# Keeping the bf16 parts of queries and keys in DRAM in the row order of the product

## The reference, cut to what matters

```
query = heads(ct_q @ Wu_q + b) + heads(rope(ct_q @ Wq_r + b))     # 16 heads of 8
key   = heads(ct_kv @ Wu_k + b) + heads(rope(x @ Wk_r + b))
value = heads(ct_kv @ Wu_v + b)
attn  = softmax(query @ key^T / 12)                               # no mask, 1024 x 1024 a head
out   = (attn @ value) @ Wo + b
```

## Time and profile before

| | |
|---|---|
| median of 3 runs | 2129.98 us (2129.47 to 2133.92) |
| the profiled execution's own time | 2124.84 us |
| span of that execution | 2123.1 us |
| busy: TensorE, VectorE, ScalarE, GpSimd | 86%, 69%, 52%, 30% of the span |
| mean granted TensorE clock | 0.939 of 2.4 GHz |
| maxima of the second attention | first at 1204.8 us, last at 1904.8 us |

### The profile page before, as it was taken

The page is one execution under the profiler, slowest core; times in us unless marked ns, Lnnn a source line. Parts: engine busy times, 40 slices in busy tenths (PEclk is TensorE's granted clock), DMA queues, the critical chain, the costliest instruction groups (busy, mean ns, idle before and its releaser), DMA issues. The chain is left out here.

```text
span 2123.1 us, 32719 instructions
## 1 busy us (share of the span) xinstructions
PE 1816.8 (86%) x12025; PEld 651.2 (31%) x12025; DVE 1473.0 (69%) x3100; ACT 1108.6 (52%) x1385; POOL 633.8 (30%) x771
## 2 busy tenths in 40 slices
PE   6455799999999999999599868888888888887899
PEld 3113333333333333333233312111211211112566
DVE  5874666666666666663344589999999899993543
ACT  4403244454444444445224248778877778885332
POOL 0031445554544454532025003303302400000152
PEclk9776699999999999999799969999999999999699
DMA  4000000000000000000021001111111111103114
GB/s 128 0 1 1 1 12 22 26 27 22 22 22 22 22 22 32 23 27 27 20 107 50 30 8 62 59 42 42 64 55 46 67 47 42 42 27 104 65 32 138
DMA packets 59451, 85.29 MB, mean 40 GB/s; under 512 B 21828, under 2 KB 38468, under 8 KB 59164
## 3 DMA queue, kind: packets, MB, share of 16 engines
q1 hardware_dynamic: 57724, 79.52, 11.1%
q0 software_dynamic: 1280, 2.62, 0.4%
q10 hardware_dynamic: 288, 1.05, 0.2%
HBM read 46.10 MB, written 32.22 MB: 37 GB/s over the span
## 5 line engine op out<-in xcount | busy, mean ns | idle before, releaser
L1575 DVE TENSOR_REDUCE h_m_half<-h_ps_max 128x1 f32<-128x512 f32 x1024 | 637.9, 682 | 53.1 <-PE h_ps_max L1284 49.0
L1460 ACT ACTIVATE h_P<-h_ps_st 128x1024 f32<-128x1024 f32 x512 | 497.7, 1023 | 103.8 <-PE h_ps_st L1300 101.2
L941 ACT ACTIVATE l_P<-l_ps_st 128x1024 f32<-128x1024 f32 (+3 forms) x384 | 306.6, 809 | 293.0 <-PE l_ps_st L821 292.0
L821 PE MATMUL l_ps_st<-l_Q,l_K 64*128 64x512 f32 (+3 forms) x1536 | 330.5, 510 | 1.2 <-DMA l_Q<-l_m_row 1.2
L1019 DVE CUSTOM_DVE_ANT_0 l_masked<-l_ps_t,l_mask 128x384 bf16<-128x384 f32 (+3 forms) x512 | 230.2, 487 | 79.5 <-PE l_ps_t L779 78.0
L1284 PE MATMUL h_ps_max<-h_K,h_Q 48*128 48x512 bf16 x1024 | 205.5, 398 | 78.3 <-DVE h_m_half L1575 75.2
L1310 PE MATMUL h_ps_o<-h_P,h_V 128*9 128x512 f32 x2048 | 271.8, 603 | 0.7 <-ACT h_P L1460 0.5
L1022 DVE TENSOR_REDUCE l_m_half<-l_ps_t 128x1 f32<-128x512 f32 x256 | 164.8, 685 | 97.1 <-PE l_ps_t L779 97.0
L990 POOL TENSOR_SCALAR_AFFINE_SELECT l_P<-l_P 128x256 f32<-128x256 f32 x256 | 102.8, 406 | 381.6 <-ACT l_P L941 381.2
L1300 PE MATMUL h_ps_st<-h_Q,h_K 51*128 51x512 bf16 x1024 | 169.8, 384 | 31.1 <-DMA h_Q<-h_m_row 18.4
L1284 PEld LDWEIGHTS h_ps_max<-h_K,h_Q 48*128 48x128 bf16 x1024 | 49.6, 93 | 404.3 <-DVE h_m_half L1575 385.9
(11 more groups left out here) (387 smaller groups left out, 2207.7 us busy)
## 6 DMA issues: line engine op xcount, KB each, us to landing
sums<-l_o SPq DMA_DIRECT2D x15, 512.0 KB, 2.6
sums<-h_o SPq DMA_DIRECT2D x15, 512.0 KB, 2.6
y_rows<-zero SPq DMA_DIRECT2D x8, 512.0 KB, 4.9
h_b<-h_a SPq DMA_DIRECT2D x32, 128.0 KB, 2.0
c_W<-in_W SPq DMA_DIRECT2D x16, 256.0 KB, 5.6
c_back<-y_rows SPq DMA_DIRECT2D x16, 256.0 KB, 5.4
l_inv<-inverse_sums SPq DMA_DIRECT2D x15, 256.0 KB
l_packed<-sums SPq DMA_DIRECT2D x15, 256.0 KB
```

Of the source, the lines that this page charges most:

```text
L821: last = pe.matmul(ps_st[x % 2][:, a, 0:w], K[n // NG % 2][rows, kt * 128:(kt + 1) * 128], Q[n % NQ][rows, c, p, q0 - c * CH:q0 - c * CH + ...
L941: act.activation(P[e % PR][:, :, 0:w], ps_st[slot["s", n, i, p] % 2][:, :, 0:w], ACT.Exp, scale=0.125).then_inc(consumed, 1)
L1460: act.activation(P[e % PR][:, :, :], ps_st[x % 2][:, :, :], ACT.Exp, scale=1.0 / 12.0).then_inc(consumed, 1)
L1575: dve.tensor_reduce(m_half[:, half, 2 * p + a, qt:qt + 1], ps_max[:, t % NB, :], AX.X, ALU.max, negate=True)\
```

## The change

The stores write the parts in the order and with the repeats of `QP` and `KP`: six slots where three stood, by three DMAs of 3, 2 and 1 slots. For queries the source is one part repeated. A group's tile half (48 partitions) then comes back with one DMA of 6 slots x 8 rows. The counts that the semaphores wait for follow.

```
-    NB, PR, NBUF, NOB, NLOAD, MIX = 3, 4, 4, 4, 12, 16
+    NB, PR, NBUF, NOB, NLOAD, MIX = 3, 4, 4, 4, 4, 16
...
-    G.q1 = nc.dram_tensor("q1_parts", [B, 3, 128, T], BF16).ap()
-    G.k1 = nc.dram_tensor("k1_parts", [B, 3, 128, T], BF16).ap()
+    G.q1 = nc.dram_tensor("q1_parts", [B, 6, 128, T], BF16).ap()
+    G.k1 = nc.dram_tensor("k1_parts", [B, 6, 128, T], BF16).ap()
...
     if b:
-        eng.wait_ge((G.q_stored, G.k_stored)[u], 16 * b)
+        eng.wait_ge((G.q_stored, G.k_stored)[u], 48 * b)
...
 def keep_parts(eng, S, b, u, done, count):
     eng.wait_ge(done, count)
-    eng.dma_start((G.q1, G.k1)[u][b].rearrange("n p t -> p n t"), G.parts[u][:, :, :]).then_inc((G.q_stored, G.k_stored)[u], 16)
+    to, parts, at = (G.q1, G.k1)[u][b], G.parts[u], 0
+    for k in (3, 2, 1):
+        part = parts[:, 0:k, :] if u else parts[:, 3 - k:4 - k, :].broadcast_to([128, k, T])
+        eng.dma_start(to[at:at + k].rearrange("n p t -> p n t"), part).then_inc((G.q_stored, G.k_stored)[u], 16)
+        at += k
...
 def load_part(eng, S, n, u):
-    eng.wait_ge((G.q_stored, G.k_stored)[u], 16 * (n // NG + 1))
+    eng.wait_ge((G.q_stored, G.k_stored)[u], 48 * (n // NG + 1))
     src, to = (G.q1, G.k1)[u][n // NG], (G.Q, G.K)[u][n % G.NBUF]
     for a in range(2):
-        lo, row = 64 * a, (n % NG) * 32 + 16 * a
-        rows = src[:, row:row + 16, :].rearrange("n (r p) t -> n r (p t)", p=2)
-        for count in (3, 2, 1):
-            part = rows[0:count] if u else rows[3 - count].unsqueeze(0).broadcast_to([count, 8, 2 * T])
-            eng.dma_start(to[lo:lo + 8 * count, :, :].rearrange("x p t -> x (p t)"), part).then_inc(G.loads[n % G.NBUF], 16)
-            lo += 8 * count
+        row = (n % NG) * 32 + 16 * a
+        eng.dma_start(to[64 * a:64 * a + 48, :, :].rearrange("x p t -> x (p t)"),
+                      src[:, row:row + 16, :].rearrange("n (r p) t -> n r (p t)", p=2)).then_inc(G.loads[n % G.NBUF], 16)
```

## The result

The changed kernel takes 2111.67 us (median of 4 runs, 2109.39 to 2113.59), the kernel before 2130.36 us beside it. The ratio is 0.9908, with a 95% interval of 0.9892 to 0.9923: 18.7 us faster.

A forecast was written before the change was run, and what follows sets the result against it. VectorE was taken to set the second attention's pace, so only its idle time counts: 13.19 us (n%4 = 2) plus 3.93 (n%4 = 1), together 17.1, less 1.0, gives 16.1 off the median: 2114 us, range 2108 to 2123.

The forecast's parts named there:

- The spread: Group loads in the second attention: 6 slots over 6 engines, engine 0 carrying 128 KB a group instead of 272.
- The place worked out: Group with n%4 = 2 from 1362 us: data end at 1375.8 instead of 1380.3, and TensorE's 3.96 us stall goes.
- The new wait: At n%4 = 2 the query load waits for the doubled query store; 0.2 us missing at worst, 2.5 to spare at best.
- The rival that this landing eats the gain: Doubled query store lands at 1376.7, stalling 4.5 us instead of 3.96 three times; 2128 us, chance 0.10.
- the prediction's own limit of 1372.3: Query store's landing time in the n%4 = 2 place; from there on each us later costs one.
- the two rates that bounded the landing: Engine 0 at 16.0 or 21.7 kB/us: the doubled query store lands at 1372.5 or 1369.8; the slow one was taken.
- The issue time: SyncE's queue: 5 us less a group from 4 issues in place of 12, 0.9 more for the store; both costed at nothing.
- the place at 1362: The n%4 = 2 group with the query store: engine 0 carries 288 KB for 384, so data end 4.5 us earlier.
- The 1.0 us set aside for what might stay: Taken off the 17.1 us for what three n%4 = 2 places and the rest may keep.
- Fewer engines: Rival: 6 slots spread over only 2 engines, 7.5 us more stall in six places, 45 us, 2175 us; chance 0.05.
- the common factor with 16: Rival's rule for a load's engine count: 6 slots would give 2 engines; chance of fewer engines 0.05.
- another engine holds VectorE back at the same place: Rival: without the DMA wait TensorE or ScalarE delays VectorE; less than half of 17 us comes, about 2122; chance 0.08.

The follow-up runs named there:

- e7: Kernel before, with only the four copies of maxima issued by ScalarE after its eviction and not by SyncE; ratio 1.0494.
- e9: Kernel before, with only the four copies of maxima issued by GpSimd after its split and not by SyncE; ratio 1.0013.
- e5: Changed kernel, but each tile half loaded by three transfers of 2 slots: 12 issues a group, 2 engines wide; ratio 1.0373.
- e8: Changed kernel, but each tile half loaded by two transfers of 3 slots: 8 issues a group, 3 engines wide; 2140.92 us, ratio 1.0047.
- e3: Changed kernel with the load's source dimensions swapped, 8 rows outermost: 4 issues a group, 8 engines wide; ratio 0.9901.
- e4: Changed kernel's doubled store with the loads of the kernel before: 12 issues a group, 3 and 2 engines wide; ratio 1.0075.
- e1: Changed kernel, but each tile half loaded by three transfers over column ranges: 12 issues a group, still 6 engines wide; ratio 0.9926.
- e2: Kernel before, single store and 12 issues kept, with only the load's source dimensions swapped: 8 rows outermost, 8 engines wide; ratio 0.9905.

## Why the prediction was right

**The bound.** VectorE's idle time is what could be gained, as forecast: 18.1 us less of it made the stage 18.0 us shorter. The table above bears this out over nine kernels. In e7 and e9, where other engines issue the copies, stage less idle time is 694.3 and 689.5 us, so there it holds less closely.

**The spread.** 6 slots over 6 engines, 128 KB on engine 0: the share was 0.38 (0.37 forecast). The place worked out had its data end at 1376.2 (1375.8 forecast), the scores at 1377.84. The outer dimension set the width in e5, e8, the change and e3, for 2, 3, 6 and 8. The Trainium skill (DMA: Bandwidth & Descriptors, Why a DMA increments its semaphore by 16) has the same widths by its rule for the engine count; these runs agree.

**The new wait.** Forecast between 1369.8 and 1372.5, the query load came at 1371.19, 9.0 us after the first store. The rival that this landing eats the gain did not come. It is a real price, though: e4 shows a doubled store at 17.5 us when nothing else shrinks, and e1 the same place losing 2 us to four more issues. By the prediction's own limit of 1372.3 the margin was 1.1 us, and the two rates that bounded the landing, 1369.8 and 1372.5, did not settle on which side of it the landing would fall.

**The issue time.** I costed SyncE's issues at nothing. For the sum that did no harm, since the store's three issues took 1.99 us for 0.45 (I had 0.9 more, it was 1.5), and the query loads 1.43 in place of 3.69. But e1 shows that the nothing was a balance of a longer landing and fewer issues behind it: with 12 issues kept, 7.2 us of the stage's gain are gone. The prediction gave the whole gain to the spread; in the presence of the doubled store some 7 of the 18 us hang on the fewer issues. This part of the mechanism the prediction used in its sum for the place at 1362 (two query issues behind the wait) but did not name as a source of the gain. In e2, with a single store, the twelve issues cost nothing.

**The size.** 16.1 us forecast, 18.0 in the stage. The 1.0 us set aside for what might stay was not needed, an idle gap of 0.3 us of VectorE at 1599 had been left out, and the rest, 0.6 us, lies in smaller gaps. The 18.7 us of the medians are the stage's 18.0 and 0.7 that no view explains, which is less than a measurement tells. That the forecast of 2114 us came near 2111.67 also rests on taking the 16 us off the median: the profiled execution lay 5.5 us under it, most likely because its last stage lacked the wait told of above, which the forecast had no way to know. That part was luck.

**The rivals.** Fewer engines was made real in e5 and e8: the direction held, and 3 engines lie near the point of decision, on the side of a loss. The price for 2 engines, 45 us for 80.5, was short by nearly half, as neither the places without a store nor what comes beside the waits had been counted. The form of this rival that was put up, the common factor with 16, was already excluded by its own rows: it would give 1 engine for the transfer of 3 parts, and a share of 0.20 is 3. That another engine holds VectorE back at the same place did not come: with the waits gone the idle time fell from 53.1 to 35.0 us, where this rival had it stay near 50.

## What to carry to other kernels

When a tiny transfer is late, look at how wide the transfers ahead of it are, and not only at the total: at a DMA share of 0.12 to 0.2 the engines look idle in the mean, while two or three of them carry all of the load. Look at the outermost dimension of the DRAM side: outermost dimensions of 2, 3, 6 and 8 gave shares of 0.13, 0.19, 0.38 and 0.48 here. Swapping two dimensions in a `rearrange`, with the broadcast slices to match (e2), gives what the new layout gives, without twice the bytes in DRAM. Before making a store larger to make a load simpler, look at who waits for the store, and what is queued behind the wait.

## What the runs showed of the hardware

A queue of their own (e9) hardly shortened the copies' way past a load: 4.6 us at most to landing beside a median of 1.7.

After TensorE's three waits over 3 us in the kernel before, its granted clock was down to 0.50, 1.2 GHz, no later than 0.6 us after its return. Two waits of nearly the same length show what this costs: in the worked place TensorE stood 2.00 us in e1 and 2.19 us in e9. In e1 the clock stayed at 1.00; in e9 it fell to 0.50 about a microsecond after the return. VectorE, e1 and then e9:

```profile
1378.48 10.01 DVE L1575 TENSOR_REDUCE h_m_half<-h_ps_max 128x1 f32<-128x512 f32 x16 [1.52 <-PE h_ps_max L1284]
```

```profile
1384.51 5.78 DVE L1581 TENSOR_REDUCE h_m_half<-h_ps_max 128x1 f32<-128x512 f32 x9 [1.05 <-PE h_ps_max L1284]
```

In e1 VectorE is busy without a gap for 10 us after its idle time of 1.52 us. In e9, after one of 1.71 us and two reductions, it stands another 1.05 us, as it stood 0.97 us behind the 4.11 in the kernel before. So with the fallen clock a wait cost about a microsecond more here. Why the clock fell in one of these two cases and not in the other the runs don't show.

Three stores of 3, 2 and 1 slots, 1.5 MB, let their load go 9.0 us after the first was issued beside other traffic, where one of half the size took 7.25.
